# A graph network kernel: the sums by source carried in two chains and stored once, and the beginning put in another order

## The reference

```python
h = max(layernorm(x), 0)
# layer 0: attention without softmax
h2 = (h @ W.T).reshape(N, 4, 32)
att = leaky_relu(a_src . h2[src] + a_dst . h2[dst], 0.2)      # per edge and head
x = x + segment_sum(att * h2[src], dst)
h = max(layernorm(x), 0)
# layer 1: gated messages, summed by the SOURCE of the edge
e = concat([h[src], h[dst], edge_attr])
m = relu(e @ W_weight + b_weight) * sigmoid(e @ W_gate + b_gate)
x = x + segment_sum(m, src)
```

## Time and profile before

| | |
|---|---|
| runs | 5301.56, 5303.04, 5309.51 us |
| profiled execution | 5309.96 us, of which the span is 5308.1 |
| mean granted clock of TensorE | 0.893 |
| busy in the span | TensorE 3995.3 us (75%), POOL 3618.5 (68%), DVE 3600.1 (68%), ACT 2164.3 (41%) |
| DMA | 839.91 MB, 158 GB/s in the mean; 72 to 82 GB/s in the attention stage, 166 to 185 in the scatter stage, 297 to 323 in the loop by src |

### The profile page before, as it was taken

The page is one execution under the profiler, slowest core; times in us unless marked ns, Lnnn a source line. Parts: engine busy times, 40 slices in busy tenths (PEclk is TensorE's granted clock), DMA queues, the critical chain, the costliest instruction groups (busy, mean ns, idle before and its releaser), DMA issues.

```text
span 5308.1 us, 125356 instructions
## 1 busy us (share of the span) xinstructions
PE 3995.3 (75%) x33743; PEld 3157.7 (59%) x33743; DVE 3600.1 (68%) x8423; ACT 2164.3 (41%) x5076; POOL 3618.5 (68%) x3857
## 2 busy tenths in 40 slices
PE   6776666566666666698988898988898867888882
PEld 4465555555555555476666666666666655666662
DVE  7998777777777777654444444444444438999996
ACT  4122222222222222254444444444444436887782
POOL 5777777777777777577777777777777773444441
PEclk9888888888888888799999999999999989999996
DMA  5333333333333333365555555555555559999998
GB/s 156 105 82 80 76 75 76 78 76 76 78 76 76 78 75 76 72 185 171 169 170 169 170 168 171 169 171 166 169 168 168 170 154 297 323 323 316 318 321 312
DMA packets 474828, 839.91 MB, mean 158 GB/s; under 512 B 123831, under 2 KB 302289, under 8 KB 474526
## 3 DMA queue, kind: packets, MB, share of 16 engines
q1 hardware_dynamic: 238977, 438.31, 27.2%
q0 software_dynamic: 170192, 354.21, 24.4%
q10 hardware_dynamic: 65620, 46.95, 2.7%
HBM read 545.33 MB, written 300.16 MB: 159 GB/s over the span
## 4 chain that ended last, share of the span: by engine, by line
POOL 44%; issue 20%; DMA 17%; DVE 7%; PE 7%; ACT 3%; POOLq 1%; ACTq 1%; SPq 0%; DVEq 0%
POOL parts L616 18%; POOL gat L601 13%; POOL rows L601 13%; DMA parts<-rows,sidx 8%; DMA rows<-parts 6%; ACT rows L1102 2%; DVE gat L1714 2%; PE ps L855 1%; PE ps L723 1%; PE ps L857 1%; PE ps L924 1%; DVE msg L1722 1%; PE ps L937 1%; DMA out_x<-rows 1%; DVE msg L1509 1%
## 5 line engine op out<-in xcount | busy, mean ns | idle before, releaser
L616 POOL DMA_INDIRECT parts<-rows,sidx x1664 | 1627.8, 978 | 547.2 <-issue 451.3
L765 PE MATMUL ps<-msg,to_node 128*128 128x128 f32 x3328 | 609.0, 358 | 743.4 <-DVE msg L1509 743.4
L855 PE MATMUL ps<-w_edge,gat 128*128 128x256 f32 x3328 | 1049.5, 399 | 0.0
L765 PEld LDWEIGHTS ps<-msg,to_node 128*128 128x128 f32 x3328 | 562.7, 263 | 765.2 <-issue 765.2
L601 POOL DMA_INDIRECT gat<-table,sidx x832 | 793.4, 954 | 260.6 <-issue 257.5
L601 POOL DMA_INDIRECT rows<-table,sidx x832 | 792.0, 952 | 253.6 <-issue 249.9
L1102 ACT ACTIVATE rows<-ps 128x512 f32<-128x512 f32 x832 | 481.5, 607 | 1033.1 <-DMA parts<-rows,sidx 920.2
L857 PE MATMUL ps<-hot,to_edge 128*128 128x256 bf16 x4992 | 842.0, 279 | 0.0
L1060 ACT ACTIVATE earlier<-ps,less_three 128x512 bf16<-128x512 f32 x416 | 263.4, 684 | 1194.6 <-PE ps L774 1147.5
L857 PEld LDWEIGHTS ps<-hot,to_edge 128*128 128x128 bf16 x4992 | 503.2, 101 | 286.7 <-issue 29.7
L855 PEld LDWEIGHTS ps<-w_edge,gat 128*128 128x128 f32 x3328 | 550.6, 202 | 51.6 <-issue 18.5
(11 more groups left out here) (247 smaller groups left out, 7592.8 us busy)
## 6 DMA issues: line engine op xcount, KB each, us to landing
rows<-parts SPq DMA_DIRECT2D x208, 1028.0 KB, 7.8
ea<-in_edge_attr SPq DMA_DIRECT2D x422, 256.0 KB
parts<-rows,sidx POOLq DMA_INDIRECT x1664
nodes_w<-table_a SPq DMA_DIRECT2D x416, 64.0 KB, 5.3
gat<-table,sidx POOLq DMA_INDIRECT x832
rows<-table,sidx POOLq DMA_INDIRECT x832
x1w<-x ACTq DMA_DIRECT2D x208, 64.0 KB
x<-x1o ACTq DMA_DIRECT2D x208, 64.0 KB
```

The lines of the kernel that those rows point to most:

```text
L616: nc.gpsimd.indirect_dma_start(out=parts, out_offset=bass.IndirectOffsetOnAxis(ap=sidx[:, s, j:j + 1], axis=0), in_=rows[:, s, j, :], in_o ...
L765: mmi = pe.matmul(out_ps, to_node[:, s % 2, j * P:(j + 1) * P], msg[:, s % 2, j * F:(j + 1) * F], start=(j == 0), stop=(j == J - 1))
L855: pe.matmul(z, eat[:, s % 2, j // 4, (j % 4) * P:(j % 4 + 1) * P], w_edge[:], start=True, stop=False)
```

## The change

- **Loop by src.** The edges in the order by source are cut into two halves; side 0 of group g is now the g-th 512 edges of the first half, side 1 the g-th of the second, so each side walks through the nodes in one chain. A node that is not finished in a group is carried: TensorE adds the evicted `sums` of the group before, shifted by the step between the two windows, into the sums of this group, with one 64x64 matmul for each side (`shifter`, made by POOL two groups ahead). Rows that are finished are stored once: POOL adds the rows of `x1` to them and writes 128 rows by one indirect DMA to `out`, where the unfinished rows get an address that the bounds check leaves out (`NOWHERE`). At the end the last 64 rows of the first chain, which the second chain's beginning shares, are added by one accumulating DMA.
- **Tables.** `x1` becomes the third column block of `table_a` (now 384 floats wide), so that a side load brings 1536 bytes a row instead of 1024, with the row of `x1` in it. `late`, `later` and `latest`, their zero fills and the final adding are gone. New are 52 copies of 242 rows from `x1` to `out` in the scatter stage. The first pass copies one more piece of 125 rows from `out` back to `x1` ahead of its first side loads.
- **Waits.** SP's side loads wait for POOL's addition four groups before; the side loads of the first four groups stand ahead of the wait for the last scatter. PE waits for the shifter, POOL for the store four groups before.
- **Beginning.** SP's first four x tiles stand ahead of the edge lists; ACT loads first what the node stage needs, then the biases and the weights of layer 1; the constants are made in another order; DVE's eviction of the weights stands behind its first scaling; the stores of `table0` go one tile ahead of those of the scores; the last store of scores is awaited by SP and ACT, no longer by POOL. `group_limits` does without the two masking operations.
- **Histogram.** One instruction of DVE makes the one-hot rows of two groups (104 instead of 208), and DVE and TensorE take turns on two pairs of slots.

```diff
+        table_a = dram("table_a", [N + P, 3 * F])
+        x1 = table_a[:, 2 * F:3 * F]
...
 # SP, beginning
+            for s in range(XU):
+                load_nodes(s, s)
             sp.wait_ge(consts, N_PADS)
...
-            for k in range(LAST):
-                sp.dma_start(last_rows(x1, k), last_rows(x, k)).then_inc(x_copied, 16)
+            for k in range(PIECES):
+                sp.dma_start(piece(x1, k), piece(x, k)).then_inc(x_copied, 16)
...
 # SP, scatter stage, once for each of 52 turns
+                    sp.dma_start(out[bass.ds(i * ZERO, ZERO), :], x1[bass.ds(i * ZERO, ZERO), :]).then_inc(out_copied, 16)
...
 # SP, loop by src
+            def load_ahead(v, q, g):
+                sp.wait_ge(pre_up, 2 * (q + 1 + U))
+                sp.sem_inc(past_waits, 1)
+                load_rows(g + U, v % U)
+                sp.wait_ge(final_up, 2 * q + 10)
+                sp.sem_inc(past_waits, 1)
+                load_sides(g + U, (v + U) % V)
...
+                for s in range(U):
+                    load_sides(s, s)
+                sp.wait_ge(all_placed, 1)
+                for s in range(U):
+                    load_rows(s, s)
...
 # POOL, loop by src
+            def shift_of(q, g, slot):
+                nc.gpsimd.tensor_copy(step_s[:, slot:slot + 1], step_to[:, bass.ds(g, 1)]).then_inc(step_up, 1)
+                pool.wait_ge(step_up, q + 1)
+                pool.sem_inc(past_waits, 1)
+                nc.gpsimd.tensor_scalar(shifter[slot], iota_s, step_s[:, slot:slot + 1], None, ALU.is_equal).then_inc(shift_up, 1)
+
+            def store_sums(v, q, g, turn, ahead):
+                s = v % U
+                if ahead:
+                    pool.wait_ge(sum_up, q + 4)
+                    pool.sem_inc(past_waits, 1)
+                    shift_of(q + 2, g + 2, (v + 2) % U)
+                pool.wait_ge(stored[s], 16 * (2 * turn + v // U) + 16)
+                pool.sem_inc(past_waits, 1)
+                nc.gpsimd.tensor_copy(target_s[:, s:s + 1], target[:, bass.ds(g, 1)]).then_inc(final_up, 1)
+                pool.wait_ge(copied2, 2 * q + 4)
+                pool.wait_ge(aw_in[s], 32 * (2 * turn + v // U + 1))
+                pool.sem_inc(past_waits, 1)
+                nc.gpsimd.tensor_tensor(final[s], sums[v], a_win[v][:, 2 * F:3 * F], ALU.add).then_inc(final_up, 1)
+                pool.wait_ge(final_up, 2 * q + 18)
+                pool.sem_inc(past_waits, 1)
+                nc.gpsimd.indirect_dma_start(
+                    out=out, out_offset=bass.IndirectOffsetOnAxis(ap=target_s[:, s:s + 1], axis=0),
+                    in_=final[s], in_offset=None, bounds_check=N - 1, oob_is_err=False).then_inc(stored[s], 16)
...
+                for s in range(U):
+                    pool.wait_ge(stored[s], 16 * (w * GU + GU) + 16)
+                pool.wait_ge(joint_up, w + 1)
+                pool.sem_inc(past_waits, 1)
+                pool.dma_start(out[bass.ds(first, H), :], joint[0:H, :], accum_op=ALU.add).then_inc(joint_added, 16)
...
 # TensorE, loop by src, behind L937
+                if carried:
+                    pe.wait_ge(shift_up, q)
+                    pe.sem_inc(past_waits, 1)
+                    for a in range(2):
+                        mmi = pe.matmul(ps[a * H:(a + 1) * H, 2 + a, 0:F], shifter[(v - 1) % U][a * H:(a + 1) * H, :],
+                                        sums[(v - 1) % V][a * H:(a + 1) * H, :], start=False, stop=True)
                 mmi.then_inc(sum_up, 1)
...
 # DVE, histogram
-                for s in range(U):
-                    dve.wait_ge(hist_ps, U * i + s + 1)
-                    one_hot_once(s, U * i + s).then_inc(hist_hot, 1)
+                for s in range(2):
+                    dve.wait_ge(hist_ps, 2 * i + s + 1)
+                    one_hot_once(s, U * i + 2 * s).then_inc(hist_hot, 1)
```

More of the change, by code:

```diff
@@ L24 @@
 H = P // 2
+NOWHERE = 1 << 20
 LOW = 512
@@ L688, in limits @@
             def limits():
+                pe.wait_ge(weights_later, N_LATER)
+                pe.matmul(ps[:, 7, 0:2 * F], ones[0:1, :], bias_row[:], start=True, stop=True)
                 pe.wait_ge(once_up, 1)
@@ L948, in _ @@
-            with pe.Fori(0, passes2) as w:
-                for s in range(U):
-                    by_src_step(s, w * G + s, w * GU, True)
-                with pe.Fori(0, GU - 1) as i:
-                    turn = pe.snap(w * GU + i + 1)
-                    for s in range(U):
-                        by_src_step(s, U * turn + s, turn, False)
-                add_sources(U - 1, w * G + G - 1, w * GU + GU - 1)
-                for s in range(1, U):
-                    sum_rows(s, w * G + G - U + s)
+                                        msg[:, s % 2, at:at + F], start=(u == 0), stop=(u == J // 2 - 1 and not carried))
@@ new lines, in _ @@
+            with pe.Fori(0, passes2) as w:
+                for v in range(V):
+                    by_src_step(v, w * G + v, w * GV, True)
+                with pe.Fori(0, GV - 1) as i:
+                    turn = pe.snap(w * GV + i + 1)
+                    for v in range(V):
+                        by_src_step(v, V * turn + v, turn, False)
+                add_sources(V - 1, w * G + G - 1, w * GV + GV - 1)
+                for v in range(V - 3, V):
+                    sum_rows(v, w * G + G - V + v, True)
+                pe.wait_ge(copied2, 2 * (w * G + G) + 2)
+                pe.wait_ge(shift_up, w * G + G)
+                pe.sem_inc(past_waits, 1)
+                pe.matmul(ps[0:H, 2, 0:F], shifter[(G - 1) % U][0:H, :], sums[V - 1][0:H, :], start=True,
+                          stop=True).then_inc(joint_ps, 1)
@@ L1375, in nodes @@
                 ids_of_gathers()
+                for s in range(V):
+                    next_gather(s, s)
                 key_of(0)
@@ L1424, in _ @@
             nodes()
-            for s in range(V):
-                next_gather(s, s)
             key_of(1)
@@ L1735, in _ @@
             with dve.Fori(0, passes2) as w:
-                windows(2, w, 2 * w + 1)
+                sides(w, 2 * w + 1)
                 for s in range(U):
```

355 lines of the change are left out of this document (190 added, 165 removed).

## The result

The changed kernel takes 5262.85 us (median of four runs, 5257.84 to 5275.49) against 5304.51 of the kernel before on the same chips: ratio 0.9924, 95% interval 0.991 to 0.9937. Faster, then, by 42 us or 0.8%, where 92 us were forecast, and the time lies 5 us outside the range. The profiled execution has a span of 5264.6, 43.5 less than before.

| stretch | before | after | difference | forecast |
|---|---|---|---|---|
| start to POOL's 65th gather | 205.6 | 218.0 | +12.4 | 0 |
| to the loop's first load of `rows` | 4184.0 | 4177.4 | -6.6 | +2 |
| to the end of the last eviction of sums | 829.7 | 850.7 | +21.0 | -14 (-12 and -2) |
| to the end of the span | 88.8 | 18.5 | -70.3 | -80 |

A forecast was written before the change was run, and what follows sets the result against it. Most of the span is POOL issuing indirect DMAs; the loop by src is bound by DMA, close above DVE. End -80, loop -12, around it -2, scatter +2, beginning 0 give -92: median 5303.04 to 5211, range 5180 to 5258.

The forecast's parts named there:

- The loop: Loop by src: period from 3.896 to 3.84 us a group, -12 us in all (-35 to +30).
- Net 64.8 + 2.1 - 5.4 = 61.5, 5% less: Loop's DMA engine-us a group: longer side rows add 2.1, store replacing accumulation saves 5.4; DMA alone then needs 3.70 us.
- about 2.7 of 3.9 us, off the path: Loop: POOL's work a group, one indirect DMA, four small operations and handshakes, said not to set the pace.
- DVE's floor: Loop: DVE alone would take 3.73 us a group, unchanged; DMA costs 0.17 over it, 35 us in all.
- a third of the rest: Loop: with limits 3.70 and 3.73 so close, only a third of the gap is gained: 3.84 us, 12 in all.
- The carried matmuls: Loop, TensorE: two 64x64 matmuls a group take 0.27 us, mostly covered; at most 56 us if not.
- rival (1): Less gain: copy on 5 engines delays attention 20 to 74 us, or loop stays on DMA or SP; 5230 to 5285, chance 0.20.
- a copy on 5 engines: Beginning: copying x to `x1` over 5 engines would take 62 to 147 us, up to 74 late; forecast took it as hidden.
- Rival (3): Slower: POOL's new operations hold up DVE's L1722 and L1707 in the loop, or cost like casts; 5327 to 5410, chance 0.06.
- Both signs: Prediction wrong if the loop takes over 3.95 us a group, or the attention stage starts 10 us late.
- The end: After the last eviction of sums: 88.8 us become 9 (6 to 14), saving 80 (75 to 83).
- The beginning: First 200 us: 0 (-10 to +10); terms -3 + 3 - 2.4 + 0 - 1.2, with nothing taken for the histogram.

The follow-up runs named there:

- e5: The kernel before with the accumulating DMAs of the loop by src left out, so the sums are not stored: 5276.18 us, loop 796.9.
- e9: As e6, with the indirect store of each group left out: 5208.29 us, loop 799.4.
- e6: The changed kernel with the lighter POOL of e1 and the 1024-byte side loads of e3 together: 5234.30 us, loop 816.3.
- e1: The changed kernel with steps copied for eight groups, targets for four, shifter between addition and store on POOL: 5249.39 us, ratio 0.9892, loop 835.6.
- e3: The changed kernel with side loads of 1024 bytes a row; POOL adds other columns instead of x1: 5235.52 us, loop 816.0.
- e2: The changed kernel with POOL's addition of x1 done twice for each group: 5323.63 us, loop 900.7.
- e11: The changed kernel with e1, e4 and e7, 1024-byte side loads and an accumulating indirect store replacing POOL's addition: 5217.74 us, ratio 0.9839, loop 827.9.
- e10: As e6, with the carried matmuls left out, waits and shifters kept: 5216.47 us, loop 808.2.
- e4: The changed kernel with the histogram of before, one DVE instruction for each group and four slots: 5259.15 us, 65th gather at 210.22.
- e7: The changed kernel with ACT handing over the x buffers ahead of its weight loads: 5261.01 us, 65th gather at 213.51.
- e8: The changed kernel with four small transfers on SP after the joint store, each waiting for the one before: 5268.74 us.

## Why the prediction was wrong

**The loop: the step that failed.** Two terms failed. In the sum of the DMA, "Net 64.8 + 2.1 - 5.4 = 61.5, 5% less", the 2.1 for the longer side rows was too small and the rows of `parts` were put at no change; and POOL's "about 2.7 of 3.9 us, off the path" was neither 2.7 nor without cost. The runs give the costs one by one, along a path from before to after:

| step | loop, us | difference |
|---|---|---|
| before | 829.7 | |
| the sums' DMAs away (e5) | 796.9 | -32.8 |
| two chains, carried matmuls, shorter POOL chain; no store, narrow sides (e9) | 799.4 | +2.5 |
| the indirect store (e6) | 816.3 | +16.9 |
| wide side loads (e1) | 835.6 | +19.3 |
| POOL's chain as in the change | 850.7 | +15.1 |

(The order matters: coming from e3, the wide side loads cost 34.7 and POOL's chain nothing. The +2.5 is less than can be read.)

First, the DMA. The traces record single packets; this is the mean time of one, in ns, from 4500 to 4800:

| kernel | share of 16 engines | row of `parts`, 4112 bytes | side row | sums or store |
|---|---|---|---|---|
| before | 1.04 | 188 | 52 (1024 bytes) | 70 (512 bytes) |
| e5 | 0.94 | 194 | 48 (1024) | |
| e6 | 0.96 | 197 | 50 (1024) | 88 (2064) |
| e1 | 1.03 | 202 | 83 (1536) | 98 (2064) |
| the change | 1.03 | 203 | 83 (1536) | 98 (2064) |

A side row is a row of `table_a` in a side load. A group has 128 of them and 256 rows of `parts`. In engine-us (one of the 16 engines busy for a us) the longer side rows cost 128 x (83 - 52) ns = 4.0, where I took 2.1 (between nothing and 3.1). The rows of `parts` cost 256 x (203 - 188) ns = 3.8, where I put nothing. The store costs 2.6% of 16 x 300 us over 77 groups, 1.6, where I took 4. With these the sum is 64.8 + 4.0 + 3.8 - 9.4 + 1.6 = 64.8: nothing is gained, and DMA alone needs 3.90 instead of 3.70, as measured in this stretch. (With full engines in both kernels the total has to come out so; new are the single prices.) That a side row costs 83 ns is not only a sign of full engines: in e2, at a share of 0.92 (4950 to 5200), it takes 80. Why the rows of `parts` take longer than before in every variant stays open. It isn't the number of packets beside them, for before has the most.

Counting bytes would have come nearer: before, 1.25 MB in 3.896 us are 320 GB/s, and the change's 1.27 MB need 3.97 us at that rate. It isn't a law either: e11 moves 1.21 MB in 3.90 us, 311 GB/s.

Second, the gain of taking the sums away is capped by DVE's floor (-33 of the -35 that the prediction allowed), but the additions are not: with them the landing of `rows` goes from 6.0 (e5) to 7.5 us (e1, 4500 to 4800). I set gains and additions off against each other below a floor, and took a third of the rest.

Third, POOL's chain was mis-sized: 3.36 us unhindered, of which 0.88 is the wait for its own addition and 0.46 the shifter, and up to 4.21 beside DVE. That it costs 15 us is shown by e1; by which path is not. From about the 110th group on the store comes some 4.9 us after the eviction has begun, where it had come after 2.2 to 2.5; in e1 it is back at 2.2 soon after. From 4850 to 5150 the packets are slower in the change (side rows 91 ns, the store's 139) than in e1 (83 and 102), and ACT waits for `rows`, not for POOL. So it may be that a store issued at another moment of the group slows the loads; no run tried that alone.

The carried matmuls took 0.44 us in the loop where 0.27 was put; e10 gives them some 8 us.

**The rivals.** The time lies where rival (1) put it (5230 to 5285), and for half of its reason: the loop's DMA engines stayed full, at 3.96 a group on average for the first 140 groups. That it said 3.97 is luck: it came from a store at 7.6 (measured: 1.6) and side rows at 3.1 (4.0). Its other half, a copy on 5 engines, did not happen. Rival (3) had the right two engines and the wrong victim: DVE's operations kept their length in the loop, POOL's did not. Nor was it right that the trace of before has no overlap long enough to test this. In its beginning DVE's L1334, which has two inputs in SBUF and takes 0.16 us alone, met the last of POOL's casts (they ran from 12.37 to 19.64) and ended with it to within 0.13 us:

```profile
19.02 0.49 DVE L1334 SCALAR_TENSOR_TENSOR shifts<-mv,rstd 128x4 f32<-128x4 f32 x1
```

Both signs that the prediction gave for being wrong came: over 3.95 us a group, and an attention stage 10 us late.

**The end: -70 for -80.** The mechanism held. I gave 2.5 us for "semaphores and the end of the program"; there were 8.7 behind the last landing, and 7.2 instead of about 3 before the joint store, since POOL was behind.

**The beginning: +12.4 for 0.** The histogram, which I put at nothing between -7.6 and +4, cost 9 (e4: 7.8). The order of the loads cost 5 (e7), with the chain that the prediction described; of its 5 us I let 3 through, and set an earlier start of DVE against it. That start was won (first tile at 11.84 instead of 15.71) and lost again at ACT's wait for the fills and at L1398, which took 3.91 us instead of 0.60 beside POOL's casts. From the end of the histogram to the 65th gather about 2 us were gained (1.2 forecast).

**Between the two.** From the 65th gather to the loop's first load 6.6 us went. The twelve kernels that are built on the change lie between 4171.8 and 4181.0, the two that are built on the one before at 4184.0 and 4187.3 (e5), so a gain of this stretch is there, and its size is known to a few us. The zero fills that left the attention stage, forecast at nothing, are a candidate; that wasn't tried.

## To carry to other kernels

When a stage's DMA engines are full, a transfer that gets longer is not nearly free because no packet is added: here a row half as long again cost 83 ns instead of 52. If no row of that size is in the trace, let the range reach beyond the mean price of a byte. What is taken away is capped by the next limit, and what is added is not. An engine that gets small operations must be costed as a chain, with its own semaphore waits and with the neighbour that holds it up. And what is moved to the front of a queue gains only if the wait at its head is moved too.

## What the hardware showed that I had not expected

- Issuing a copy as 1250 rows of 512 bytes kept SP busy 5.3 us a piece (53.18 for ten); as whole blocks it was 0.81.
- The roles of DVE and POOL turn round: in the loop POOL's copy waits for DVE (0.84 instead of 0.20), in the beginning two DVE operations wait for POOL's casts (3.91 instead of 0.60).
- After POOL's last landing 8.7 us passed in which the trace shows nothing (3.5 in e9, without the indirect stores), and some 5 us of SP's work beside them were free (e8).
- A row of 1536 bytes in the side loads took 80 to 83 ns in the mean (91 in the change's later stretch), one of 1024 bytes 48 to 52.
